# A graph network on one core: ScalarE's copy of a block's new keys and values, placed ahead of its wait for the maxima

## What is computed

```python
xn = layernorm(h) * ln1_g[l] + ln1_b[l]
q, k, v = xn @ wq[l] + bq[l], xn @ wk[l] + bk[l], xn @ wv[l] + bv[l]   # 8 heads of 32
scores = (q[dst] * k[src]).sum(-1) / sqrt(32)        # an edge to itself is added for every node
m = segment_max(scores, dst); ex = exp(scores - m[dst])
agg = segment_sum(ex / z[dst] * v[src], dst)          # z is the segment sum of ex
h = h + agg @ wo[l] + bo[l]
h = h + gelu((layernorm(h) * ln2_g[l] + ln2_b[l]) @ w1[l] + b1[l]) @ w2[l] + b2[l]
```

## Time and profile before

| | |
|---|---|
| median of 3 runs | 4810.94 us (4806.27 to 4817.87) |
| the profiled execution | 4814.66 us, of which the profile's span is 4812.9 us |
| PE busy | 3632.3 us (75%) |
| DVE busy | 3577.2 us (74%) |
| POOL busy | 3096.6 us (64%) |
| ACT busy | 1888.9 us (39%) |
| mean granted TensorE clock | 0.831 of full |

### The profile page before, as it was taken

How to read it: one execution, slowest core, us unless ns; L and a number is a source line. 1 busy time by engine, 2 the same in 40 slices (tenths; PEclk the granted TensorE clock), 3 DMA queues, 4 the chain that set the end, 5 groups by cost and what they waited for, 6 DMA issues and landing times. The chain is left out here.

```text
span 4812.9 us, 99366 instructions
## 1 busy us (share of the span) xinstructions
PE 3632.3 (75%) x17128; PEld 2684.0 (56%) x17129; DVE 3577.2 (74%) x5494; ACT 1888.9 (39%) x4155; POOL 3096.6 (64%) x2969
## 2 busy tenths in 40 slices
PE   8874448888899999378888999995656666666666
PEld 6431236666676676256666666774445555544544
DVE  6732267777788885477888888873799898888866
ACT  3442213344444455033444454553333333334343
POOL 0052167777777773577777777763677777777653
PEclk9886768999999999588999999997777776666766
DMA  3452556777777673577766777763566655655542
GB/s 119 161 164 70 141 162 199 223 214 207 209 230 218 206 223 118 155 212 217 224 208 203 238 228 218 220 184 96 162 174 194 178 171 173 182 167 162 143 141 70
DMA packets 384186, 864.68 MB, mean 180 GB/s; under 512 B 160913, under 2 KB 173671, under 8 KB 384118
## 3 DMA queue, kind: packets, MB, share of 16 engines
q0 software_dynamic: 232080, 680.08, 48.8%
q1 hardware_dynamic: 151720, 183.05, 11.4%
q10 hardware_dynamic: 318, 0.84, 0.1%
HBM read 791.89 MB, written 143.30 MB: 194 GB/s over the span
## 5 line engine op out<-in xcount | busy, mean ns | idle before, releaser
L1243 POOL DMA_INDIRECT kv<-kv_dram,idx x2616 | 2745.3, 1049 | 966.5 <-issue 723.9
L1795 PE MATMUL ps_acc<-kv,ident 128*128 x5232 | 1341.4, 421 | 54.1 <-DVE kv L1412 39.8
L1795 PEld LDWEIGHTS ps_acc<-kv,ident 128*128 128x128 f32 x5232 | 1107.9, 215 | 316.2 <-issue 140.1
L1307 DVE TENSOR_TENSOR kv<-kv,ps_q 128x1024 f32 x654 | 786.4, 1215 | 270.0 <-DMA kv<-kv_dram,idx 235.7
L1312 DVE TENSOR_REDUCE sc<-kv 128x32 f32 (+2 forms) x654 | 784.0, 1211 | 15.6 <-DVE kv L1307 13.1
L1412 DVE TENSOR_TENSOR kv<-kv,ps_q x654 | 753.2, 1214 | 3.0 <-DVE sm L1536 3.0
L1623 ACT COPY agg<-ps_acc 128x256 f32<-128x256 f32 x147 | 54.8, 372 | 1437.1 <-issue 735.4
L1789 PE MATMUL ps_acc<-acc_scaled,ident 128*128 128x256 f32 x306 | 147.4, 578 | 428.0 <-DVE acc_scaled L1376 428.0
L1846 PE MATMUL ps_big<-xnaT,w_ffn 128*128 128x128 f32 x3136 | 375.7, 278 | 2.8 <-ACT xnaT L1686 2.8
L1846 PEld LDWEIGHTS ps_big<-xnaT,w_ffn 128*128 128x128 f32 x3136 | 359.5, 193 | 14.7 <-issue 3.5
L1859 PE MATMUL ps_w<-w_ffn,shared 128*128 128x256 f32 x1568 | 364.6, 386 | 0.0
(11 more groups left out here) (215 smaller groups left out, 4798.8 us busy)
## 6 DMA issues: line engine op xcount, KB each, us to landing
rec_dram<-rec_out SPq DMA_DIRECT2D x98, 512.0 KB, 4.3
rec_in<-rec_dram SPq DMA_DIRECT2D x98, 512.0 KB, 5.4
kv<-kv_dram,idx POOLq DMA_INDIRECT x2616, 3.7
rec_by_node<-rec_in SPq DMA_DIRECT2D x49, 512.0 KB
windows<-kv SPq DMA_DIRECT2D x49, 384.0 KB, 2.4
kv_dram<-rec_in SPq DMA_DIRECT2D x49, 256.0 KB
rec_out<-in_x SPq DMA_DIRECT2D x48, 128.0 KB
w_ffn<-in_L_gnn_w SPq DMA_DIRECT2D x4, 1024.0 KB, 6.5
```

The costliest lines, as they stand in the source:

```text
L1243: pool.indirect_dma_start(kv[:, u * W + slot, :], None, kv_dram[l], bass.IndirectOffsetOnAxis(ap=idx[:, u, slot:slot + 1], axis=0), bounds ...
L1307: nc.vector.tensor_tensor(at, at, q, ALU.mult).then_inc(s["mul"], 1)
L1795: mm = nc.tensor.matmul(ps_acc[:, 0:D], ident[:], at[:, :, slot, :].rearrange("p a d -> p (a d)"), start=False, stop=False, skip_group_che ...
```

## The change

ACT's three copies of `record` are parted. The copy of keys and values and the copy of row numbers make up `record_kv(b - 3)`, placed in ACT's iteration after `turn_sums(b - 1)` and before the exponential of block b. They wait for a new semaphore `kv`, which the last matmul of `next_kv` raises, and they raise a new semaphore `kvout`. The copy of the query part stays where it was, behind the wait for `qkv`. In layers 0 and 1 POOL's scatter and PE's next `next_kv` wait for `kvout` in place of `recq`. No instruction that computes or moves data is added or removed. Layer 2 has no `record`, and its scatter still waits for `recq`.

```diff
--- before.py
+++ after.py
@@ -1061,7 +1061,7 @@
         between = {name: sem(name) for name in (
             "mul", "score", "relk", "to_exp", "exped", "scaled", "weighted", "summed", "acc", "agg", "round", "start",
             "norm", "residual", "second", "scale1", "scale2", "aggT", "aggTs", "w", "var1", "sd1", "var2", "sd2", "rs1", "xn1", "xT1", "xTs1", "f1", "g", "f2", "rs2", "xn2", "xT2", "xTs2", "qkv", "recq", "types", "typesT", "typesTs", "pairs", "away", "onehot", "relp", "relrow", "outx", "last",
-            "used", "taken", "query", "node", "zsum", "zinit", "evened")}
+            "used", "taken", "query", "node", "zsum", "zinit", "evened", "kv", "kvout")}
         numbers = sorted(handle.num for handle in between.values())
         assert numbers[-1] - numbers[0] == len(numbers) - 1
         for l in range(3):
@@ -1195,7 +1195,7 @@
 
                 @block.gpsimd
                 def _(pool):
-                    summed, recorded = Passed(pool, s["summed"]), Passed(pool, s["recq"])
+                    summed, recorded = Passed(pool, s["summed"]), Passed(pool, s["recq" if typed else "kvout"])
                     scattered = Passed(pool, s["scat"], 16)
 
                     def scatter(b):
@@ -1720,13 +1720,16 @@
                                                            bias=query[:, c:c + 1])
                         ins.then_inc(s["xTs2"], 1)
 
+                    def record_kv(b):
+
+                        act.wait_ge(s["kv"], b + 1)
+                        nc.scalar.copy(flat(rec_out[:, one(b % OUT_RING), 0:2 * D]), ps_kv)
+                        nc.scalar.copy(scatter_to[:, one(b % OUT_RING)], flat(node_rank[:, one(b), 0:1])).then_inc(s["kvout"], 1)
+
                     def record(b):
 
-                        to = rec_out[:, one(b % OUT_RING), :]
                         act.wait_ge(s["qkv"], b + 1)
-                        nc.scalar.copy(flat(to[:, :, 0:2 * D]), ps_kv)
-                        nc.scalar.copy(scatter_to[:, one(b % OUT_RING)], flat(node_rank[:, one(b), 0:1]))
-                        nc.scalar.copy(flat(to[:, :, 2 * D:3 * D]), ps_w[:, 0:D]).then_inc(s["recq"], 1)
+                        nc.scalar.copy(flat(rec_out[:, one(b % OUT_RING), 2 * D:3 * D]), ps_w[:, 0:D]).then_inc(s["recq"], 1)
 
                     def iteration(b):
                         if exists(b - 1):
@@ -1739,6 +1742,8 @@
                             start(b, counts[3])
                         if exists(b - 1):
                             turn_sums(b - 1)
+                        if exists(b - 3) and not typed:
+                            record_kv(b - 3)
                         if exists(b):
                             def whole(k, chunk0, filled):
                                 if typed:
@@ -1866,9 +1871,9 @@
                     def next_kv(b):
                         pe.wait_ge(s["xTs2"], b + 1)
                         if not isinstance(b, int) or b:
-                            pe.wait_ge(s["recq"], b)
+                            pe.wait_ge(s["kvout"], b)
                             settle(pe)
-                        project_kv(l + 1, xnbT)
+                        project_kv(l + 1, xnbT).then_inc(s["kv"], 1)
 
                     def next_q(b):
                         if not isinstance(b, int) or b + 1 < NB:
```

## The result

The changed kernel takes 5063.98 us (median of 4 runs, 5062.47 to 5067.04) against 4809.09 us (4 runs, 4806.27 to 4817.87). The ratio is 1.0526, 95% interval 1.0513 to 1.0538: 255 us slower. The forecast was 5056 us.

A forecast was written before the change was run, and what follows sets the result against it. It took POOL's pace to bound blocks of four to six chunks, with a PE, ACT and DVE loop just under. Added waits and lost clock summed to +245 us on 4814.66 less 3.7, giving 5056 us, range 4950 to 5150.

The forecast's parts named there:

- What bounds: Layers 0 and 1: POOL paces blocks of four to six chunks; a PE, ACT and DVE loop lies just under, 22.24 us.
- Item 1: ACT behind the norms: the two copies leave, worth 0 now, 0.56 us per block at most.
- Item 2: ACT waits for keys and values before the maxima; 5.64 us to the transposes, was 1.90; serial loop 25.98 us, four chunks.
- Items 3 and 4: PE's loop: each chunk fewer takes 1.73 us off; the clock falling in PE's idle time adds 1.3 us per block.
- Item 5: Blocks against present pace: four chunks +3.87 and +3.82, three +5.50 and +5.10, five +0.4, six 0; +245 us in all.
- Item 6: POOL's scatter freed up to 5 us earlier, worth 0; SP's stores and PE's next keys and values also 0.
- The drains: Last iterations, without exponential: the square root also waits for keys and values, some 2 us each; left out, under 10 us.
- the clock does not follow: PE's clock: the serial loop holds but the clock's part is 0; 4975 us, chance 15%.
- every block starts its sums at the low clock: PE's sums: 3.03 us lost in each block, 1.73 above forecast in 84 blocks; 5201 us, chance 8%.
- faster: ACT: copies fall into its wait for late maxima, saving 0.56 us behind the norms in 92 blocks; 4759 us, chance 4%.
- no difference: ACT's wait for keys and values is short because POOL's lead covers it; 4811 us, chance 5%.

The follow-up runs named there:

- e10: The change with its new semaphores, but the two copies put back behind the norms: 4812.36 us against 4814.86 for the kernel before, ratio 0.9996.
- e6: The kernel before with one additional copy of keys and values behind the norms: 6738.02 against 6756.05 us, ratio 0.9981.
- e2: The change with ACT's wait kept ahead of the exponential but both copies behind the norms: ratio 1.0703 to the kernel before, beside 1.0728 for the change.
- e12: The change with 34 more matmuls per block of layers 0 and 1 in PE's idle stretch: 4982.82 against 4814.86 us for the kernel before, ratio 1.0346.
- e7: The change with POOL's scatter waiting for the query copy again: ratio 1.0712 to the kernel before, beside 1.0728 for the change.
- e1: The change with its new semaphores, the two copies back behind the norms, in the first job: 6768.31 against 6756.12 us, ratio 1.0027.
- e9: The changed kernel itself once more, beside the kernel before: 7168.55 against 6677.04 us, ratio 1.0728.

## Why the prediction was right

*What bounds.* Four- and five-chunk blocks at POOL's pace with a PE loop just under it: e10 shows the first, the changed kernel the second.

*Item 1*, worth nothing: e6.

*Item 2*, the serial loop. Forecast 5.64 us from keys and values to the transposes, measured 5.56 in every block of three to five chunks. The total was right, its inside not: I counted 0.66 for the copies and 0.15 for issue, but e2 shows some 0.55 of issue, which the copies cover. Removing the copies from that place would have saved 0.2 us, not 0.66.

*Items 3 and 4*, the chunks and the clock. Here the size was partly luck. I took the price from the five-chunk blocks, as if PE idled there for nearly 4.4 us at a stretch. It idles 3.2 to 3.4 us before the transposes there, with the query matmuls and a first pause ahead of that:

```profile
907.77 0.26 PE L479 MATMUL ps_w<-bias_parts,ones_rows 3*128 3x256 bf16 x1 [1.83 <-DVE rec_out L1484]
912.34 0.69 PE L474 MATMUL ps_t<-ident,xna 128*128 128x128 f32 x2 [3.24 <-ACT xna L1698]
```

Forecast 8.33 + 1.3 = 9.6 us for transposes and sums beyond the 0.77; measured 0.97 + 9.52 against 0.77 + 8.33, 1.39 more. The view of `ps_acc` alone, as in the earlier trace rows:

```profile
868.90:1304.20 435.30, 168.38 (x645) 0.91 0.71 213
1304.20:1794.90 490.70, 170.26 (x630) 0.88 0.64 187
1794.90:1998.60 203.70, 61.40 (x216) 0.90 0.49 149
```

170.26 / 18 = 9.46 us where 7.76 is due at full clock, and 61.40 / 8 = 7.68 for 6.03. e12 shows that this is the clock. The rival "the clock does not follow" gave 4975 us, and e12, in which it does not, measured 4983. The rival "every block starts its sums at the low clock" (5201 us) had the mechanism right and the price wrong. In all 84 blocks with five to two chunks the step from the transposes to the sums takes 0.97 us, where it takes 0.77 at full clock. In the four-chunk block shown above, the clock is at its lower level from 2.0 us before the transposes until 3.8 us into the sums, and then full:

```profile
1644.60:1651.40 6.80, 4.75 (x13) 3.42 (x14) 5.59 (x9) 3.81 (x9) 3.29 (x4) 0.50 0.53 163
1651.50:1657.15 5.65, 5.65 (x28) 4.89 (x28) 4.57 (x7) 0.00 (x0) 3.30 (x4) 1.00 0.42 139
```

So 2.0 of the 6.8 slow microseconds fall on idle time, and 1.2 us of the sums are lost where 3.03 would be by the earlier trace rows, a block whose sums take in the whole slow stretch. The Trainium skill ("TensorE: Matmul & The Clock Gate", HAM oscillation) describes kernels in which each gap between bursts makes the next burst start throttled. The trace agrees: the transposes take 0.69 us in place of 0.44.

*Item 5*, block by block: four chunks forecast +3.87 and +3.82, measured 27.26 - 23.41 = +3.85 and 27.26 - 23.46 = +3.80, together 138 us as forecast. The match to 0.02 us is two small errors that cancel: the segment is 0.08 us shorter than forecast, the clock's part 0.09 us larger. Three chunks forecast +5.50 and +5.10, measured 25.46 - 20.05 = +5.4 and +5.0, 83 for 85. Five chunks +0.4 as forecast. Two chunks 22.6 for 23.82: their segment is 5.05 us and not 5.56, and they lost 0.5 us to the clock and not 1.3; 8 us in all for the forecast 10. Six chunks 0.

*Item 6*, the scatter: e7 and e10. The drains, left out as under 10 us, cost some 7.

The rivals "faster" and "no difference" fell by the result and the stretches above, and e6 finds nothing at the place from which "faster" had its gain.

## What to carry to other kernels

An instruction is early only if what it waits for is early. On an engine that runs in order, moving a copy ahead of a critical wait puts the copy's own wait on the critical path, and in the two four-chunk blocks shown that meant 3.7 us more from keys and values to the transposes, for 0.56 us of work. Before moving it, read when its operand is ready against when the wait that it passes ends (here 1518.44 against 1515.30 us), and ask which other engine the wait leaves idle: TensorE's clock fell and took another third of the loss.

## What was not expected of the hardware

In the first three jobs the kernel before took some 40% more than the 4809 us shown at the top, with the same program. The mean durations of the main ACT, DVE and POOL instructions are the same within 1.5% (a GELU 377 ns in the trace of the kernel before and 382 in e1, a gather 1049 and 1044). ACT, POOL and DVE around one four-chunk block of e1:

```profile
2011.97 1.28 ACT L1693 ACT_TABLE_LOAD   x1
2027.79 2.18 ACT L1693 ACTIVATE shared<-ps_big,b 128x128 f32<-128x128 f32 x8 [14.54 <-remote]
```

```profile
2024.25 1.00 POOL L1243 DMA_INDIRECT kv<-kv_dram,idx  x1 [0.31 <-issue]
2029.13 1.00 POOL L1223 DMA_INDIRECT rec_in<-rec_by_node,node_at  x1 [3.88 <-issue]
```

```profile
2021.27 1.22 DVE L1312 TENSOR_REDUCE sc<-kv  x1 [6.55 <-issue]
2027.06 0.36 DVE L1362 TENSOR_TENSOR sm<-sc,meta 128x192 f32<-128x192 f32 x1 [4.57 <-issue]
```

ACT stands still for 14.54 us behind the GELU's table load, with no event in the profile that ends it ("remote"), and DVE for 6.55 and 4.57 us, with no releaser either ("issue"). DVE resumes for good at 2027.06 and ACT at 2027.79, after POOL's last gather of the block, begun at 2024.25. In the two-chunk blocks at a layer's end, where POOL has no gathers left to make, PE again takes 11.25 us from the end of the sums to keys and values, which took 28.34 in the four-chunk block shown (2008.86 to 2037.20), and some 24 with three chunks. So the stalls go together with POOL's stream of gathers; that the gathers cause them is not shown. What is held up, and why in some jobs alone, was not tried and stays open. e9, which met the longer condition, and e10 to e12, which did not, ran on chips with the same number, so it does not go by that.
